# Sandwich of linear attention and soft mixture of experts on one core: new order of the first dispatch block on three engines, and the lower halves in pieces of 256 columns on POOL

## What is computed

```python
x = x + _layernorm(attn(_layernorm(x)))       # qkv, (q k^T / 16) v without a softmax, projection, inner residual
x = x + _layernorm(ffn(_layernorm(x)))        # soft mixture of experts, 64 experts with 32 slots each
# ffn:
logits = einsum('bmd,dnp->bmnp', x, phi)
dispatch = softmax(logits, axis=0)            # over the batch, which has two entries
combine = softmax(logits over n*p, axis=-1)
slots = einsum('bmd,bmnp->bnpd', x, dispatch)
y = einsum('bnpd,nde->bnpe', slots, W) + b
out = einsum('bnpd,bmnp->bmd', y, combine)
```

## Time and profile before

| | |
|---|---|
| median of 3 runs | 640.99 us (640.54 to 641.14) |
| the profiled execution's own time | 641.88 us |
| its span | 640.1 us |
| PE busy | 628.2 us (98%), 5351 matmuls |
| DVE busy | 447.9 us (70%), 857 instructions |
| ACT busy | 359.0 us (56%), 694 |
| POOL busy | 230.2 us (36%), 410 |

### The profile page before, as it was taken

How to read it: one execution, slowest core, us unless ns; L and a number is a source line. 1 busy time by engine, 2 the same in 40 slices (tenths; PEclk the granted TensorE clock), 3 DMA queues, 4 the chain that set the end, 5 groups by cost and what they waited for, 6 DMA issues and landing times.

```text
span 640.1 us, 15341 instructions
## 1 busy us (share of the span) xinstructions
PE 628.2 (98%) x5351; PEld 395.4 (62%) x5351; DVE 447.9 (70%) x857; ACT 359.0 (56%) x694; POOL 230.2 (36%) x410
## 2 busy tenths in 40 slices
PE   8999999999999999999999999999999999999996
PEld 8898644545444444444444457777777777777776
DVE  5978888835244453446344399999888888888886
ACT  5666776843233232224444356777777777777764
POOL 5375896820000000000000001555555555555554
PEclk9999999999999999999999999999999999999999
DMA  8920032325766666666555531222222222222201
GB/s 266 402 77 1 1 67 50 67 60 156 201 176 176 177 193 185 173 178 203 135 136 186 159 104 67 91 90 90 90 90 90 90 90 90 90 90 90 90 16 34
DMA packets 78485, 77.07 MB, mean 120 GB/s; under 512 B 6386, under 2 KB 74995, under 8 KB 76147
## 3 DMA queue, kind: packets, MB, share of 16 engines
q1 hardware_dynamic: 76112, 74.48, 38.4%
q10 hardware_dynamic: 2338, 2.16, 1.0%
HBM read 51.71 MB, written 23.07 MB: 117 GB/s over the span
## 4 chain that ended last, share of the span: by engine, by line
PE 79%; DVE 8%; POOL 5%; issue 3%; DMA 2%; ACT 2%; SPq 1%; DVEq 0%; POOLq 0%; ACTq 0%
PE psL L1568 24%; PE psM L1555 11%; PE psL L1687 11%; PE psM L1705 7%; PE psM L1709 7%; PE psM L1706 7%; PE psM L1585 3%; POOL small L492 2%; DMA r_xn<-in_proj_wT 2%; PE psL L1773 1%; PE psL L1453 1%; PE psM L1511 1%; DVE phs L1091 1%; DVE small L1286 1%; DVE r_xn L1305 1%
## 5 line engine op out<-in xcount | busy, mean ns | idle before, releaser
L1568 PE MATMUL psL<-r,r_xn 128*128 128x512 f16 x768 | 176.3, 379 | 0.8 <-DVE r L1112 0.8
L1568 PEld LDWEIGHTS psL<-r,r_xn 128*128 128x128 f16 x768 | 73.4, 98 | 91.0 <-issue 7.0
L762 ACT ACTIVATE r<-psM,small 128x512 f32<-128x512 f32 x64 | 43.7, 682 | 96.3 <-PE psM L1555 95.5
L1555 PE MATMUL psM<-phs,xx 128*128 128x512 f16 (+1 forms) x384 | 93.2, 379 | 0.9 <-DVE xx L1146 0.9
L580 POOL MEMSET r_xn<- 128x8 f16 x2 | 0.3, 137 | 234.2 <-PE psL L1568 234.2
L1110 DVE TENSOR_SCALAR r<-r 128x512 f16<-128x512 f32 x64 | 28.5, 445 | 71.8 <-ACT r L762 71.8
L1687 PE MATMUL psL<-phs,r 128*32 128x512 f16 x1344 | 75.1, 379 | 0.0
L1555 PEld LDWEIGHTS psM<-phs,xx 128*128 128x128 f16 x384 | 37.3, 98 | 45.9 <-DVE xx L1146 1.4
L875 ACT ACTIVATE r<-psL,small 128x512 f32<-128x512 f32 x60 | 41.9, 776 | 37.7 <-DVE small L1313 37.4
L492 POOL TENSOR_TENSOR small<-small,epst 128x2 f32<-128x2 f32 (+3 forms) x75 | 59.8, 797 | 6.2
L1687 PEld LDWEIGHTS psL<-phs,r 128*32 128x32 f16 x1344 | 34.6, 97 | 36.5 <-issue 3.0
(11 more groups left out here) (200 smaller groups left out, 1260.8 us busy)
## 6 DMA issues: line engine op xcount, KB each, us to landing
r<-in_ffn_w SPq DMA_DIRECT2D x23, 1024.0 KB, 5.8
logit_difference<-r SPq DMA_DIRECT2D x256, 64.0 KB, 1.9
xx<-logit_difference SPq DMA_DIRECT2D x16, 1024.0 KB, 4.8
out<-r SPq DMA_DIRECT2D x32, 128.0 KB, 1.7
xres<-in_x SPq DMA_DIRECT2D x7, 512.0 KB, 11.4
r<-in_phi SPq DMA_DIRECT2D x1, 2048.0 KB, 19.3
expert_bias<-r ACTq DMA_DIRECT2D x1, 2048.0 KB, 21.6
r<-expert_bias SPq DMA_DIRECT2D x16, 128.0 KB, 5.5
```

Source lines behind the costliest of these rows:

```text
L1555: ins = mm(bk[j % 2][:, :].rearrange("p (q m) -> p q m", q=EP), xxT[:, 1, j, hx, k, :], phw[:, hp, k, :, bass.ds(nb, 1), :].rearrange("p q ...
L1568: ins = mm(psL[:, i * 512:(i + 1) * 512], x3n[:, b, j, hx, k * P:(k + 1) * P], thl[:, j % 2, hs, :], start=(j == 0 and hx + hs == 0), stop ...
```

## The change

Four things, all around block 0 of the dispatch. On POOL `x3_lo` issues two subtractions of one tile (256 columns) each in place of one of two tiles (512 columns); the first counts on POOL's own semaphore, the second on the one that says that the pair is ready. On ACT `y_squares(1, 5)` comes after `tanh(0, 0)`, `xd_hi(1)` ahead of `x3_float(0, 2)` and `d_copy(0, 0)`, and `x3_float(0, 3)` after `tanh(0, 3)` and `xd_hi(2)`. On DVE `residual(1, 2)` comes after `add_x(0, 6)`, `xd_diff(1)` and `split(0, 0)`. On PE `turn_xd(3)` comes after `d_first(5)`, and `turn_xd(4)` after `slots_first(6)`. What is computed stays the same.

```diff
--- before.py
+++ after.py
@@ -558,10 +558,12 @@
 
             def x3_lo(b, p):
 
-                t2 = slice(2 * p, 2 * p + 2)
                 pool.wait_ge(x3h_ready, X_AT[b, p] + 1)
-                nc.gpsimd.tensor_tensor(x3n[:, b, t2, 1, :], xy[:, b, t2, :], x3n[:, b, t2, 0, :],
-                                        ALU.subtract).then_inc(x3l_ready, 1)
+                for t in (2 * p, 2 * p + 1):
+                    ins = nc.gpsimd.tensor_tensor(x3n[:, b, t, 1, :], xy[:, b, t, :], x3n[:, b, t, 0, :], ALU.subtract)
+                    if t % 2 == 0:
+                        own.add(ins)
+                ins.then_inc(x3l_ready, 1)
 
             y_terms(0, 0); y_terms(0, 1); x3_terms(0, 0); y_terms(0, 2); y_terms(0, 3); x3_lo(0, 0)
             y_terms(1, 0); y_terms(1, 1); y_terms(1, 2); x3_terms(1, 0); y_terms(1, 3); x3_terms(0, 1)
@@ -799,10 +801,10 @@
             S_copy(1); T_copy(1); y_squares(0, 0); y_squares(0, 1); R_copy(1); y_squares(0, 2)
             A_copy(1); x3_float(0, 0); y_squares(0, 3); x3_hi(0, 0); y_squares(1, 0); y_squares(1, 1)
             y_squares(1, 2); y_squares(1, 3); y_squares(0, 4); x3_float(1, 0); x3_hi(1, 0); y_squares(0, 5)
-            x3_float(0, 1); xd_hi(0); x3_hi(0, 1); y_squares(1, 4); x3_float(1, 1); y_squares(1, 5)
-            act.wait_ge(phi_split, 1); tanh(0, 0); x3_float(0, 2); d_copy(0, 0); xd_hi(1); tanh(0, 1)
+            x3_float(0, 1); xd_hi(0); x3_hi(0, 1); y_squares(1, 4); x3_float(1, 1)
+            act.wait_ge(phi_split, 1); tanh(0, 0); y_squares(1, 5); xd_hi(1); x3_float(0, 2); d_copy(0, 0); tanh(0, 1)
             x3_hi(1, 1); d_copy(0, 1); x3_hi(0, 2); y_squares(0, 6); tanh(0, 2); x3_float(1, 2)
-            d_copy(0, 2); x3_hi(1, 2); x3_float(0, 3); tanh(0, 3); xd_hi(2); d_copy(0, 3)
+            d_copy(0, 2); x3_hi(1, 2); tanh(0, 3); xd_hi(2); x3_float(0, 3); d_copy(0, 3)
             x3_hi(0, 3); x3_float(1, 3); x3_hi(1, 3); tanh(0, 4); d_copy(0, 4); xd_hi(3)
             tanh(0, 5); d_copy(0, 5); x3_float(0, 4); x3_hi(0, 4); tanh(0, 6); y_squares(0, 7)
             d_copy(0, 6); x3_float(1, 4); x3_hi(1, 4); x3_float(0, 5); xd_hi(4); tanh(0, 7)
@@ -1152,7 +1154,7 @@
             bias_row(1); add_x(0, 3); residual(0, 2); add_x(1, 0); add_x(1, 1); residual(0, 3); add_x(1, 2)
             residual(1, 0); add_x(1, 3); stats_x2(1, 0); add_x(0, 4); stats_x2(0, 1); residual(1, 1)
             add_x(0, 5); xd_diff(0); stats_x2(1, 1); add_x(1, 4); stats_x2(0, 2); xd_lo(0)
-            add_x(1, 5); residual(1, 2); add_x(0, 6); xd_diff(1); split(0, 0); stats_x2(1, 2)
+            add_x(1, 5); add_x(0, 6); xd_diff(1); split(0, 0); residual(1, 2); stats_x2(1, 2)
             xd_lo(1); split(0, 1); stats_x2(0, 3); residual(1, 3); split(0, 2); xd_diff(2)
             stats_x2(1, 3); residual(0, 4); xd_lo(2); split(0, 3); residual(0, 5); xd_diff(3)
             split(0, 4); stats_x2(0, 4); residual(1, 4); xd_lo(3); split(0, 5); stats_x2(1, 4)
@@ -1623,9 +1625,9 @@
                 ins.then_inc(xhalf_done, 1)
 
             d_first(0); d_first(1); turn_xd(1); slots_first(0); d_first(2); slots_first(1)
-            d_first(3); turn_xd(2); slots_first(2); d_first(4); slots_first(3); turn_xd(3)
-            d_first(5); slots_first(4); d_first(6); slots_first(5); h_pair(1, 6); d_first(7)
-            turn_xd(4); slots_first(6); h_pair(1, 7); d_first(8); slots_first(7); turn_xd(5)
+            d_first(3); turn_xd(2); slots_first(2); d_first(4); slots_first(3); d_first(5)
+            turn_xd(3); slots_first(4); d_first(6); slots_first(5); h_pair(1, 6); d_first(7)
+            slots_first(6); turn_xd(4); h_pair(1, 7); d_first(8); slots_first(7); turn_xd(5)
             d_first(9); slots_first(8); d_first(10); slots_first(9); turn_xd(6); d_first(11)
             slots_first(10); d_first(12); slots_first(11); d_first(13); turn_xd(7); slots_first(12)
             token_sums(); d_first(14); slots_first(13); d_first(15); slots_first(14); d_tile(1, 0)
```

## The result

The changed kernel takes **642.85 us** (median of 13 runs, 642.03 to 643.52), the kernel before 641.07 beside it (13 runs, 640.54 to 641.51): a ratio of 1.0025, with an interval of 1.0018 to 1.0032. It is slower by 0.25%, where the prediction had 640.4 and a range up to 642.0. Yet the two profiled executions are nearly alike: 642.14 (span 640.3) after, 641.88 (span 640.1) before. That the medians differ by 1.8 us and the traces by 0.2 is the first thing to explain.

What follows compares the result with a forecast made beforehand. TensorE bounds the kernel, so only its stops, waiting for VectorE, can be won: 4.5 us at most. Gains mostly return as later stops, leaving 0.6: 641.88 - 0.6 = 641.3, median 640.4; own range 639.8 to 641.1, whole range 639.0 to 642.0.

Steps and rivals of the forecast that it cites:

- together 4.5 us: the most that the change can win: Six TensorE stops in the first dispatch block, all waiting for VectorE, sum to 4.5 us, the upper limit of gain.
- sum of -0.6: Net gain left at the end of the kernel: 0.6 us, taken from the profiled execution's 641.88.
- I leave 92.2: POOL's terms of (1,3), which release x3_float(1,3): end unchanged at 92.2 us, give or take 0.5.
- where the 3.2 us go again: TensorE from slots 4 to the last turn: later stops eat the earlier gains, leaving 0.6 us.
- The gain of 1.0 left over: TensorE at slots 4: start at 96.5 us, 1.0 earlier, after a stop of about 1.9 instead of 0.34.
- the step on the first tiles: VectorE's xd_diff(1) and split(0,0) come sooner, so slots(0) start at 78.1 instead of 79.23, 1.1 us earlier.
- some of POOL's waits behind VectorE: POOL ahead of the terms of (1,3): these waits go with the new order, set against 0.5 us added by four halves.
- 0.13 more on POOL: Each split lower half: two halves of 0.67 less 0.05 overlap against 1.16, 16 times, 2.1 us in all.
- rival B: POOL becomes the bound from a half of 0.73, VectorE slipping into the gaps; slots 4 0.8 later; 642.5; chance 0.13.
- The long instructions of VectorE: VectorE instructions held by POOL's lower halves: wait falls from about 0.95 to at most 0.5 us.
- Rival A: Halves cheap at 0.60 on POOL, or split(9) follows the earlier start in full: 2.0 us stays, 639.0; chance 0.22.
- in which to lose or hide this: TensorE after the last turn of the first block: no further stop, so the 0.6 us reaches the end whole.

Runs made afterwards that it cites:

- e6_pe: Kernel before with only TensorE's new list (turn 3 behind d tile 5, turn 4 behind slots 6): 641.22 us, ratio 1.0000.
- e7_act_dve: Kernel before with only the new lists of ACT and VectorE, lower halves whole: 641.82 us, ratio 1.0013 to the kernel before.
- e5_before: The kernel before, without an edit, run for a second profile: 641.04 us against 641.05, ratio 1.0000.
- e9_push_dve: e7_act_dve plus one small unused bn_stats on VectorE ahead of split(0,1): 641.53 us against 641.58 for the kernel before, ratio 1.0004.
- e11_thirteen: Kernel before (old lists) with the lower halves split for the thirteen pairs other than (1,2), (0,3), (1,3): 643.16 us, ratio 1.0031.
- e2_halves: Kernel before (old lists) with all sixteen lower halves split into two operations of 256 columns: 642.49 us, ratio 1.0021.
- e8_old_three: Kernel before (old lists) with only the lower halves (1,2), (0,3), (1,3) split: 640.23 us against 641.05, ratio 0.9986.
- e12_all_push: Kernel before with all new lists, only three lower halves split, and the small unused bn_stats of e9_push_dve: 641.31 us, ratio 0.9995.
- e3_again: The changed kernel, without an edit, run for a second profile: 643.01 us, ratio 1.0027 to the kernel before.
- e4_three: Changed kernel with only the lower halves (1,2), (0,3), (1,3) split, the others whole: 641.68 us, ratio 1.0009 to the kernel before.

## Why the prediction was wrong

**The base.** The first step, "together 4.5 us: the most that the change can win", took six stops from one execution. The one of 1.09 before d tile 4 exists only when POOL loses the meeting, and usually it doesn't. The prediction set its sum of -0.6 against that execution's 641.88, which stood 0.89 above the median, and carried the difference over to the median as it was. That is the first step that failed, by 1.15 us (590.61 less 589.46). It isn't the whole miss: with the right base the prediction would have been about 641.5, inside its range. The second step is the sum itself. It promised 0.6 less than its own base, and the changed kernel takes 0.55 more (591.16 less 590.61), so the sum is off by another 1.15 us. The first profile of the changed kernel hid 0.37 of that, since its loading ended earlier (49.10 against 49.47). The prediction saw the 0.89 and used it as a mere offset; spans of other runs would have shown it as an event.

**The sum, step by step.** Put on the clock of the first profile of before (0.37 added), the changed kernel's terms of (1,3) end at 92.70 where "I leave 92.2" had 92.22; slots 4 start at 97.22 instead of 96.5, slots 9 at 122.35 instead of 121.55, and the end of the block (token_sums) comes 0.2 later than now instead of 0.6 earlier. That is 0.5, 0.7, 0.8 and 0.8 late. So the miss begins in POOL's terms and is complete at slots 9; the last 0.3 comes at the very end, see below.

**The lists.** The part on where the 3.2 us go again was right in kind: e6_pe shows TensorE's stops moving in full. The gain of 1.0 left over was the difference to a base in which everything from d tile 4 on came 1.1 late. With that gone nothing is left, and the earlier split(0,1), which comes with the 1.1 us that the step on the first tiles counted as won, is just what loses the meeting in e7_act_dve. The change as it stands doesn't lose it (80.65 against 80.67), by 0.02 us, in either of its two profiles.

**The terms of (1,3) on POOL.** "I leave 92.2, give or take 0.5": the row says 92.14, which looks right, but where they are usually due at 90.87. That step added 4 x 0.13 = 0.5 for the halves and took it off again for "some of POOL's waits behind VectorE", for which no row was given. The half was sized well (0.67 predicted, 0.665 to 0.68 measured); the term "0.13 more on POOL" per pair was not. Pair (1,1) takes 1.67 against 1.35 in e5_before, pair (0,2) 1.85 against 1.16: 0.3 and 0.7 more: VectorE enters the gaps, and each of these four halves takes 0.85 to 0.97. Relative to add_x, the terms of (1,3) end at 43.23 in the changed kernel and 41.64 in e5_before. Of these 1.59 us, 0.46 goes with the new order of ACT and VectorE (e9_push_dve, its added instruction included) and the other 1.1 with the halves (e11_thirteen, with the old order, has 1.25 and e2_halves 1.30). That is rival B's mechanism and direction: it gave 642.5, and 642.85 was measured. That its price fits is partly luck: the 0.8 us at slots 4, which it counted from the first profile, is there only against the second (47.75 against 46.96 relative to add_x), and a part of it is the order's. What was wrong in B is its condition. It needs no half of 0.73; a gap is enough. Its chance of 0.13 came from that condition.

**The long instructions of VectorE.** Right where three lower halves follow each other: 0.8 us of slots 4, shown by e8_old_three. Only these three stand in VectorE's path; the other thirteen stand in POOL's own path to the next terms.

**The skill's figure.** From the 2.6 cycles per element in section 3.1 of the Trainium skill's GPSIMD Engine Reference the prediction had worked out, as an estimate, 0.60 for a half. The trace has 0.67, and the rows' slope of 1.92 ns a column holds. Rival A, which had halves of 0.60, is out; its other reason, that the order on VectorE would let split(9) follow the earlier start, is out with e12_all_push, where the order gives nothing.

**Behind the first block.** From there on TensorE was to have no stop "in which to lose or hide this", and that held for its stops: from the start of the last slots of the first block to the first logits of the combine it takes 209.82 us in the changed kernel (150.02 to 359.84) and in e5_before (148.99 to 358.81) alike. But the three executions with all sixteen pairs split (e2_halves, e3_again, the changed kernel) end 0.31 later behind their last TensorE work (32.03 to 32.06 us from the last group of logits to the end, against 31.73 to 31.75 in all the others). The traces place it behind all arithmetic: the last instruction on VectorE ends 2.47 before the end of the span in these three and 2.16 to 2.18 in the others, and POOL's last two semaphore instructions are 0.37 apart instead of 0.08. Thirteen split pairs (e11_thirteen) don't show it. Why POOL stands there is open; no run was made for it.

## What to carry to other kernels

Before a profile is used as a base, compare its span with the spans of other runs of the same kernel, and if it lies at their edge take a second profile: here a quarter of what could be won (1.09 of 4.5 us) wasn't usually there. Splitting an operation so that another engine gets in between is a transfer of time from one engine to the other: do it for the instances where the other engine is the late one, and leave the rest whole. And where a new order brings two instructions on one shared resource to within hundredths of a microsecond of each other, who wins is a term of the sum, and an uncertain one.

## What the hardware showed that was not expected

- A start order decided by 0.01 to 0.04 us moves the end of the kernel by 1.1 us. POOL first by 0.02 to 0.03: no loss (e5_before, the changed kernel, e6_pe). VectorE first by 0.01 to 0.04: POOL's two operations of two columns take 0.43 to 0.48 and 1.15 instead of 0.19 and 0.74. In between the starts don't tell who wins: unrounded, POOL is ahead by 0.015 or 0.016 both in e3_again, where it isn't held up, and in the first profile of before, where it is.
- In these traces the instruction that is held up ends at the release plus its own length less 0.14. In e7_act_dve, L1110 ends at 80.66, and L539 at 80.66 + 0.19 - 0.14 = 80.71, which is 80.25 + 0.46. On the other engine, in the first profile of before, POOL's lower halves end at 96.40, and L1110 at 96.40 + 0.42 - 0.14 = 96.68, which is 95.30 + 1.38.
- An added instruction with no use shortens the stretch: e9_push_dve against e7_act_dve by 0.91 us (ratio 1.0013 to 1.0004), and again e12_all_push against e4_three by 0.88 (1.0009 to 0.9995). In neither pair are the two ratios' intervals apart, but both pairs move alike, as the traces say they should.
